# Layer norm on token rows, with the inverse deviation of two norms as a power on GpSimd

## What is computed

```python
def _layernorm(x, axis=-1, eps=1e-05):
    m = jnp.mean(x, axis=axis, keepdims=True)
    v = jnp.var(x, axis=axis, keepdims=True)
    return (x - m) / jnp.sqrt(v + eps)
```

## Time and profile before

| | |
|---|---|
| median of three runs | 309.04 us (308.05 to 309.98) |
| span of the profiled execution | 308.5 us |
| that execution's place among the runs | its span is 0.5 us under their median |
| TensorE busy | 301.2 us, 98%, 3082 matmul records |
| VectorE, ScalarE, GpSimd busy | 188.7, 186.6, 157.2 us |
| chain that ended last | TensorE 91%, VectorE 4%, ScalarE 3% |
| granted TensorE clock, mean | 0.998 |

### The profile page before, as it was taken

How to read it: one execution, slowest core, us unless ns; L and a number is a source line. 1 busy time by engine, 2 the same in 40 slices (tenths; PEclk the granted TensorE clock), 3 DMA queues, 4 the chain that set the end, 5 groups by cost and what they waited for, 6 DMA issues and landing times.

```text
span 308.5 us, 7389 instructions
## 1 busy us (share of the span) xinstructions
PE 301.2 (98%) x3082; PEld 278.5 (90%) x3082; DVE 188.7 (61%) x367; ACT 186.6 (60%) x326; POOL 157.2 (51%) x144
## 2 busy tenths in 40 slices
PE   8999999999999999999999999999999999999895
PEld 7877789999998999989999999999999999987673
DVE  2685255656546778467828775664738496746862
ACT  4486337765536793357698566757567464568651
POOL 6042425863525131747868495867685886100332
PEclk9999999999999999999999999999999999999999
DMA  7969353454302331669584838384757643000002
GB/s 257 405 156 232 70 130 125 138 182 147 115 19 87 119 104 42 212 193 279 188 249 137 263 117 290 107 281 149 272 170 216 212 165 88 21 2 3 0 0 83
DMA packets 32432, 46.49 MB, mean 151 GB/s; under 512 B 6965, under 2 KB 18837, under 8 KB 32394
## 3 DMA queue, kind: packets, MB, share of 16 engines
q1 hardware_dynamic: 29994, 42.16, 43.6%
q0 software_dynamic: 960, 2.43, 2.4%
q10 hardware_dynamic: 1440, 1.38, 1.5%
HBM read 38.22 MB, written 5.71 MB: 142 GB/s over the span
## 4 chain that ended last, share of the span: by engine, by line
PE 91%; DVE 4%; ACT 3%; issue 1%; ACTq 0%; POOL 0%; DVEq 0%; POOLq 0%
PE ps L1638 22%; PE ps L1640 22%; PE ps L1639 21%; PE ps L1994 6%; PE ps L1823 3%; PE ps L1789 3%; PE ps L1660 3%; PE ps L1653 2%; PE ps L1774 2%; PE ps L1668 2%; PE ps L1646 1%; PE ps L1904 1%; PE ps L1868 1%; DVE xn_split L1412 1%; ACT w_hi L809 1%
## 5 line engine op out<-in xcount | busy, mean ns | idle before, releaser
L1638 PE MATMUL ps<-c_region,w_hi 128*128 128x224 f32 (+2 forms) x304 | 88.2, 290 | 0.7 <-DVE c_region L1082 0.7
L1640 PE MATMUL ps<-c_region,w_lo 128*128 128x224 f32 (+2 forms) x304 | 85.3, 281 | 0.0
L1639 PE MATMUL ps<-c_region,w_hi 128*128 128x224 f32 (+2 forms) x304 | 85.2, 280 | 0.0
L560 POOL TENSOR_TENSOR w_lo<-w_stage,w_hi 128x512 fp32r<-128x512 f32 x30 | 48.5, 1635 | 31.1 <-ACT w_hi L809 31.0
L1638 PEld LDWEIGHTS ps<-c_region,w_hi 128*128 128x128 f32 x304 | 58.1, 191 | 1.8 <-DVE c_region L1082 1.2
L1639 PEld LDWEIGHTS ps<-c_region,w_hi 128*128 128x128 f32 x304 | 58.1, 191 | 0.3
L1640 PEld LDWEIGHTS ps<-c_region,w_lo 128*128 128x128 f32 x304 | 58.0, 191 | 0.0
L809 ACT ACTIVATE w_hi<-w_stage 128x1024 fp32r<-128x1024 f32 (+1 forms) x42 | 49.7, 1196 | 2.6 <-DVE v_region L1484 2.6
L1082 DVE TENSOR_TENSOR c_region<-s_region,c_region 128x448 fp32r<-128x448 f32 (+1 forms) x44 | 37.3, 848 | 17.5 <-ACT c_region L936 11.6
L567 POOL TENSOR_TENSOR w_lo<-w_stage,w_hi 128x512 fp32r<-128x512 f32 x28 | 37.9, 1384 | 8.3 <-ACT w_hi L809 8.3
L1638 PE MATMUL ps<-xn_split,w_hi 128*128 128x296 f32 x128 | 40.2, 314 | 0.5 <-DVE xn_split L1082 0.4
(11 more groups left out here) (183 smaller groups left out, 573.4 us busy)
## 6 DMA issues: line engine op xcount, KB each, us to landing
w_stage<-in_w_gate SPq DMA_DIRECT2D x17, 512.0 KB, 4.2
w_stage<-in_w_up SPq DMA_DIRECT2D x17, 512.0 KB, 4.5
w_stage<-in_w_down SPq DMA_DIRECT2D x7, 1024.0 KB
expert_rows<-blank_rows SPq DMA_DIRECT2D x4, 448.0 KB, 3.5
v_region<-in_blocks SPq DMA_DIRECT2D x6, 272.0 KB, 4.0
w_stage<-in_w_down SPq DMA_DIRECT2D x3, 512.0 KB
v_region<-expert_rows SPq DMA_DIRECT2D x1, 1344.0 KB, 8.3
expert_out<-v_region ACTq DMA_DIRECT2D x6, 224.0 KB, 4.4
```

The lines of the kernel that those rows point to most:

```text
L560: w = g.tensor_tensor(wl[:, r], ws[:, r], wh[:, r].bitcast(F32), ALU.subtract)
L1638: mm(o, a_h, b_h, start=start, stop=False)
L1639: mm(o, a_h, b_l, start=False, stop=False)
L1640: return mm(o, a_l, b_h, start=False, stop=stop)
```

## The change

The residual is transposed by TensorE to rows of tokens (`turn_in`, three tiles of 128, 128 and 40 tokens per half, six transposes); VectorE takes mean and variance of each tile with `bn_stats` and `bn_aggr` (`sums`), one number per token and partition, and normalises a tile with one `tensor_scalar` (`normal`). TensorE transposes the rows back (`turn_back`), and VectorE copies them from PSUM (`take_back`, `take_halves`, `take_spread`); `high` and `low` read PSUM directly. In layers 0 and 1 ScalarE's `root` stays, on three columns. In layers 2 and 3 GpSimd adds epsilon and raises to the power -0.5 (`inverse_deviation`), and only one load of the sigmoid table is left. The normalised rows of layer 1 are the token rows that are scattered to the experts, so `turn_tokens` and its copies go. Tokens are tiled by halves, six tiles in place of five (TT = 6, TA = 3), with one more pair of scatters and of fetches. Some steps move: `logits(0, ...)` goes behind `gate_up(0, 0)` and `turn_in(1, 1)`, `take_logits` and `rank_experts` for the first half go into unit 0, the low part of the first half of the shared down weight goes to GpSimd, `back_mul(3)` goes ahead of `sums(2, 0)`, and a DMA of the identity is issued between the two late patch loads.

```diff
-TT = NT // P
-TA = NC // P
+TA = -(-NC // P)
+TT = TA * C
...
+                if i == 0:
+                    sp.dma_start(cb[:, 0:CB_TRI], const[:, 0:CB_TRI]).then_inc(s["d_ident"], 16)
...
             for k in range(KD):
                 if k == 1:
+                    pool.wait_ge(s["dn0_hi"], 1)
+                    for o in range(2 * W1, 2 * W1 + W1 // 2, 512):
+                        d = g.tensor_tensor(wl[:, o:o + 512], ws[:, o:o + 512], wh[:, o:o + 512].bitcast(F32), ALU.subtract)
+                    d.then_inc(s["dn0_lo"], 1)
                     pool.wait_ge(s["gate_mul"], 1)
...
+            def inverse_deviation(L, c):
+                n = nth(L, c)
+                r = slice(n * TA, (n + 1) * TA)
+                pool.wait_ge(s["ln_mv"], (n + 1) * TA)
+                g.tensor_scalar(rstd[:, r], pat(mv[:], n * TA * 2 + 1, [2, TA]), EPS, None, ALU.add).then_inc(s["ln_log"], 1)
+                pool.wait_ge(s["ln_log"], n + 1)
+                g.tensor_tensor(rstd[:, r], rstd[:, r], power[:, 0:TA], ALU.pow).then_inc(s["ln_rs"], 1)
+
+            inverse_deviation(2, 0)
+            inverse_deviation(2, 1)
+            inverse_deviation(3, 0)
+            inverse_deviation(3, 1)
             for c in range(C):
                 for m in range(KD):
-                    pool.wait_ge(s["ln_xn"], 8 + 2 * c + m)
+                    pool.wait_ge(s["ln_xn"], 7 + 2 * c + m)
...
                 scale_second(4)
                 back_silu(3)
+                sigmoid_tables()
+                scale_second(5)
                 back_high(2)
-                square(2, 0)
                 back_high(3)
...
-            log_exp_tables()
-            root(2, 0)
-            sigmoid_tables()
             delta(0, 0)
-            square(2, 1)
-            log_exp_tables()
-            root(2, 1)
-            sigmoid_tables()
             delta(0, 1)
             delta(1, 0)
             delta(1, 1)
-            log_exp_tables()
-            square(3, 0)
-            root(3, 0)
             previous(0, 0)
-            square(3, 1)
             previous(0, 1)
-            root(3, 1)
             previous(1, 0)
             previous(1, 1)
             relu_first(0)
-            sigmoid_tables()
...
+            def sums(L, c):
+                for i in range(TA):
+                    n, j = tokens(i), TA * nth(L, c) + i
+                    dve.wait_ge(s["ln_turn"], C * nth(L, c) + i // 2 + 1)
+                    v.bn_stats(bn[0:n, j * 6:(j + 1) * 6], row_bank(L, c, i)[0:n, :]).then_inc(s["ln_bn"], 1)
+                for i in range(TA):
+                    n, j = tokens(i), TA * nth(L, c) + i
+                    dve.wait_ge(s["ln_bn"], j + 1)
+                    v.bn_aggr(mv[0:n, 2 * j:2 * j + 2], bn[0:n, j * 6:(j + 1) * 6]).then_inc(s["ln_mv"], 1)
...
+                dve.wait_ge(s["ln_rs"], nth(L, c) + 1)
+                for i in range(TA):
+                    n, j = tokens(i), TA * nth(L, c) + i
+                    v.tensor_scalar(row_tile(L, c, i), row_bank(L, c, i)[0:n, :], mv[0:n, 2 * j:2 * j + 1],
+                                    rstd[0:n, j:j + 1], ALU.subtract, ALU.mult).then_inc(s["ln_row"], 1)
+
+            def take_back(L, c):
+                dve.wait_ge(s["ln_back"], nth(L, c) + 1)
+                v.tensor_copy(chunk(xnf[:], c, NT), turned_back(L, c)).then_inc(s["ln_xn"], 1)
...
                 if u == 0:
-                    centre(1, 1)
-                    shared_down_low(0, s["dn0_hi"], s["dn0_lo"])
+                    sums(1, 1)
+                    take_logits(1, 0, TA)
+                    rank_experts(0, TA)
+                    shared_low(0)
                 if u == 1:
-                    shared_low(0)
+                    normal(1, 1)
                     rows(1, 0, TA)
-                    normal(1, 1)
                     shared_low(1)
                 if u == 2:
                     low(1, 1)
+                    take_back(1, 1)
...
-            centre(2, 1)
+            sums(2, 1)
             add_state(0, 0, state(0, 0, inject(0, 0)))
             normal(2, 1)
             add_state(0, 1, state(0, 1, inject(0, 1)))
+            take_halves(1)
             scan10 = state(1, 0, inject(1, 0))
-            centre(3, 0)
+            sums(3, 0)
             in11 = inject(1, 1)
             add_state(1, 0, scan10)
             scan11 = state(1, 1, in11)
             v.memset(pat(xnf[:], 0, [T + 1, KD * B]), 0.0)
+            normal(3, 0)
             add_state(1, 1, scan11)
-            normal_spread(0)
-            centre(3, 1)
+            take_spread(0)
+            sums(3, 1)
             mix(0, 1, 0)
             mix(0, 0, 0)
+            normal(3, 1)
             mix(0, 1, 1)
             mix(0, 0, 1)
-            normal_spread(1)
+            take_spread(1)
...
-            logits(0, TA, 3)
             half_ready(0, 0)
             pe.wait_ge(s["ln_lo"], 3)
             gate_up(0, 0)
-            mean(1, 1)
-            turn_tokens(0)
+            turn_in(1, 1)
+            logits(0, TA, 2)
             gate_up(0, 1)
             positions(0, TA, 2)
-            variance(1, 1)
...
                 if u == 2:
+                    turn_back(1, 1)
                     pe.wait_ge(s["dn0_lo"], 1)
-                    pe.wait_ge(s["xt_ok"], 1)
+                    pe.wait_ge(s["rows_set"], 1)
...
                 gate(0, 0, 0)
-                mean(2, 1)
+                turn_in(2, 1)
                 gate(0, 1, 0)
-                variance(2, 1)
                 gate(0, 0, 1)
                 gate(0, 1, 1)
+                turn_back(2, 1)
                 gate(1, 0, 0)
                 gate(1, 1, 0)
                 gate(1, 0, 1)
-                mean(3, 0)
+                turn_in(3, 0)
                 gate(1, 1, 1)
-                variance(3, 0)
-                mean(3, 1)
+                turn_back(3, 0)
+                turn_in(3, 1)
                 keep_clock(8, 1)
-                variance(3, 1)
+                turn_back(3, 1)
```

More of the change, by code:

```diff
@@ L543, in _ @@
             g.memset(zero[:], 0.0).then_inc(s["const_set"], 1)
-            g.memset(ones[:], 1.0 / D).then_inc(s["const_set"], 1)
+            g.memset(mv[:], 1.0).then_inc(s["const_set"], 1)
+            g.memset(power[:], -0.5).then_inc(s["gap_set"], 1)
             g.memset(eps[:], EPS).then_inc(s["const_set"], 1)
@@ L754, in _ @@
             columns_high(1, 1)
-            square(0, 1)
             columns_high(0, 1)
@@ L818, in _ @@
                 piece_high(n, 0)
-            square(1, 0)
             root(1, 0)
@@ L1145, in _ @@
             patch_low(FULL + 1, 1, SPLIT0 + 2)
-            centre(0, 0)
+            dve.wait_ge(s["const_set"], 2)
+            sums(0, 0)
             patch_low(FULL + 2, 1, SPLIT0 + 3)
             patch_low(FULL + 3, 1, SPLIT0 + 4)
+            normal(0, 0)
             columns_low(2, 1, 1)
@@ L1156, in _ @@
             columns_low(1, 0, 1)
-            centre(0, 1)
+            sums(0, 1)
             columns_low(0, 0, 1)
+            normal(0, 1)
             v_evac(0)
-            normal(0, 1)
             v_evac(1)
@@ L1410, in find_slots @@
                     for st in range(ST):
-                        for b, at, c, n0, n1 in SPREAD:
-                            w = v.tensor_scalar(hot(st, c, n0, n1), bank(b, n1 - n0, at),
+                        for c in range(C):
+                            w = v.tensor_scalar(hot(st, c), bank(4 + c, NC),
                                                 rcb[:, RB_SLOT + st:RB_SLOT + st + 1], None, ALU.is_equal)
@@ L1683, in _ @@
             embed(0, 1)
-            pe.wait_ge(s["const_set"], 3)
+            pe.wait_ge(s["d_ident"], 16)
             pe.wait_ge(s["cls_set"], 1)
-            mean(0, 0)
+            turn_in(0, 0)
             embed(1, 1)
@@ L1718, in _ @@
             value_full(0, 0)
-            mean(0, 1)
+            pe.wait_ge(s["bias_ev"], 1)
+            turn_in(0, 1)
             pe.wait_ge(w_lo[2], 1)
@@ L1724, in _ @@
             value(1, 0)
-            variance(0, 1)
             value(1, 1)
-            pe.wait_ge(s["bias_ev"], 1)
+            turn_back(0, 1)
             pe.wait_ge(s["d_const"], 16)
@@ L1832, in _ @@
             output(0, 1, 0, HP // 2)
-            mean(1, 0)
+            turn_in(1, 0)
             output(0, 1, HP // 2, HP)
-            output(1, 1, 0, 1)
-            variance(1, 0)
-            output(1, 1, 1, HP)
+            output(1, 1, 0, 5)
+            turn_back(1, 0)
+            output(1, 1, 5, HP)
             def gate_up(e, u):
@@ L2129, in gathered_expert, with down_and_turn @@
                     down(3).then_inc(s["g_y"], 1)
-                def variance_and_down():
-                    variance(2, 0)
+                def down_and_turn():
                     back_down(2)
+                    turn_back(2, 0)
                 for e in range(1, NX):
@@ L2142, in _ @@
                 back_gate_up(3)
-                mean(2, 0)
+                turn_in(2, 0)
                 back_down(0)
```

(2 more changed lines are left out.)

277 lines of the change are left out of this document (122 added, 155 removed).

## The result

The changed kernel takes 324.73 us (median of four runs, 323.84 to 328.99) against 308.75 us for the kernel before beside it (four runs): ratio 1.0517, 95% interval 1.047 to 1.0564. The profiled execution took 324.14 us, its span is 322.2 us, 13.7 us more than before. The forecast was 315.3 us, 308.0 to 319.5: the direction was right, the forecast loss of 6.3 us less than half of the measured 16.0.

A forecast was written before the change was run, and what follows sets the result against it. TensorE, busy 98% and 91% of the chain, bounds the kernel, except the last 40 us, where the chain leaves for ScalarE and VectorE. 308.5 + 0.6 (experts) + 5.7 (tail) = 314.8, forecast 315.3 us with 0.5 from span to median; range 308.0 to 319.5.

The forecast's parts named there:

- `mixr_mul` behind the last power: Fourth norm, second half: GpSimd's two first-half products, 1.29 us each, come after the last power and hold the first mix.
- a wait at `positions`: Second layer: TensorE arrives at 107.9 and waits 1.2 us for VectorE's run of work ending at 109.0.
- six table loads: ScalarE's loads of 1.28 us each in the tail shrink to one, off the chain; worth less than they look.
- the drain that the Trainium skill counts: ScalarE table switch: the skill counts 2.66 us with a 1.38 us drain; the prediction saw no drain in the rows.
- rival 1: TensorE's clock falls before the projections: 2 us lost, 317.3 us, up to 319; chance 0.18.
- The pair: GpSimd's add and power on three columns in the third and fourth norm: taken as 0.6 us for both.
- The bound above (2.6 us): Upper bound for GpSimd's add and power together: twice the 1.29 us of a strided 296-wide `tensor_scalar`.
- The third norm's first half: Waits of about 0.65 us (tile 5) and 0.6 us (`normal`) use up TensorE's saving: first gate 0.2 us late.
- the copy behind the state: Third norm, second half: `take_halves(1)` behind the state holds the gates; the last add ends 3.2 us later.
- The second layer: Waits at `positions` and for `rows_set` delay the second logits; +0.6 us at the experts for both layers, bounds -2.0 and +2.0.
- the move of the down weight's split to GpSimd: First half of the shared down weight goes from VectorE to GpSimd, busy 51% of the span: costs nothing.
- The late first call: Under rival 4 (chance 0.10): by the skill, `inverse_deviation(2,0)` would come some 5 us late, sum near 320 us.

The follow-up runs named there:

- the mended kernels: tail_mended, and the changed kernel with ScalarE's roots, copy ahead of the state, GpSimd's split moved and zero matmuls in the waits: 322.42 us, ratio 1.035.
- before_no_keep: The kernel before without its eight zero matmuls between mean(3,1) and variance(3,1): ratio 0.999.
- roots_on_scalar: Changed kernel with logarithm and exponential on ScalarE, with table changes, in place of GpSimd's power: 317.93 us, ratio 1.0365.
- 1, 2, 3 and 6: Experiment numbers of no_pair (ratio 1.0332), roots_on_scalar (1.0365), clock_kept (1.0393) and front_only (1.0148).
- clock_kept: Changed kernel with zero matmuls added in TensorE's waits of the tail: 320.14 us, ratio 1.0393.
- mixr_first: Changed kernel with GpSimd's two mixr_mul products for the first half ahead of the last power: 320.44 us, ratio 1.0376.
- no_pair: Changed kernel without GpSimd's add and power of third and fourth norm, inverse root not computed, for timing alone: 317.86 us, ratio 1.0332.
- front_only: First two layers, tokens, merge and spread as in the changed kernel, third and fourth norm as in the kernel before: 313.31 us, ratio 1.0148.
- tail_mended: Changed kernel with mixr_mul ahead of the last power, copy ahead of the state, GpSimd's split moved, zero matmuls in the waits: 325.42 us, ratio 1.0404.

## Why the prediction fell short

The account, from the two profiles and the mended kernels (us, T to `project(0,3)` unless said):

| part | worked out as | us | predicted |
|---|---|---|---|
| up to the second layer's `turn_in` | 105.39 - 105.26 | 0.1 | 0.2 |
| second layer to T | 164.20 - 162.13 | 2.1 | 0.4 |
| orders on VectorE and GpSimd, clock of the gates | 35.48 - 31.45 | 4.0 | } |
| power in place of roots, orders mended | 31.45 - 29.17 | 2.3 | } 5.7 |
| rows and six-tile layout in place of transposed statistics | 29.17 - 25.16 | 4.0 | } |
| clock of the projections | 13.55 - 12.24 | 1.3 | 0 |

The forecast was 9.7 us short of the measured loss. The table has 7.5 of them: 4.6 us from T to `project(0,3)`, 1.3 in the projections and 1.6 ahead of T.

The first two rows are the weak ones. The first mark lies between 103.4 and 105.5 us in the profiles of kernels that do the same on TensorE up to there, so 0.1 is nothing. And the profile of the kernel before was some 1.6 us longer than its median run; since T to `project(0,3)` is 25.16 us in `before_no_keep` too, this surplus lies most likely ahead of T, and the loss there nearer 4 than 2.2 us; this is an estimate, since no second profile of the kernel before shows it. By the same surplus one step of the sum was wrong that has nothing to do with the change: I added 0.5 us to get from the span to the time, and it is 1.9 us (322.2 to 324.14).

**Right.** The direction and its first reason: VectorE's order takes the place of ScalarE's chain. `bn_stats` three in 1.08 us, `sums` 1.3 us against 1.5; `mixr_mul` behind the last power; `normal` and the copy at about their price; a wait at `positions`; six table loads worth nothing (`roots_on_scalar` has all six and is 4.7 us faster). The load is followed by the logarithm at once again (272.07 + 1.28, then 273.36), so the drain that the Trainium skill counts (ScalarE: Activation LUTs, What ACT_TABLE_LOAD costs) does not show here either.

**Failed step: the clock, priced as a rival alone, came together with the forecast.** I wrote that the largest gap near the end was 0.66 us and that no row shows what a broken stretch does, and left it out of the sum (rival 1 gave 2 us, for the projections alone). But my own steps made waits of 0.6 to 2.7 us. The runs: 1.7 us at the gates, 1.3 us at the projections, and 0.9 to 2.4 us behind `positions` (165.1 to 166.6 us from the second layer's `turn_in` to T in the four profiles of 1, 2, 3 and 6, 164.2 without a fall); `clock_kept` gets 3.8 us back. The falls at the gates and behind `positions` were not in the rival at all. A case that follows from the forecast's own waits belongs in its sum.

**The pair was a mis-sized term**: 1.2 to 2.1 us for 0.6. The bound above (2.6 us) held, the choice near the lower end did not: I scaled with the number of elements, but the power of three columns took 0.88 us or more, longer than the 0.69 us of two operands of 296 columns. At `normal(3,1)` more is lost, since `mixr_mul` waits behind it: `mixr_first` gets 1.6 us of the chain back, `roots_on_scalar` and `no_pair` 5 us with the clock.

**The third norm's first half was the second**: +0.2 us predicted for the first gate. It starts 9.5 us after T instead of 7.2: waits of 0.72 us (tile 5) and 1.31 us (`normal` behind the pair) in place of 0.65 and 0.6, and transposes back of 0.9 us where I took 0.55. Of the 2.3 us 0.65 come with the layout alone (the same mark in `front_only`); I had given merge and spread 0.2 us or less. So the second half's `normal` was late by itself, and the copy behind the state, my largest term (3.2 us), held only 0.7 us.

**The second layer**: the wait at `positions` was 2.0 us for 1.2. I costed the move of the down weight's split to GpSimd at nothing because GpSimd is busy half the time; by moving the next split onto VectorE's ranking it cost 1.1 us there, though only 0.3 us at T. And the work that TensorE was spared became waiting for VectorE.

**The late first call and the transposes.** The first power took 1.78 us and the second 0.88 us, and it started 0.08 us behind the end of the add (272.01 + 0.26, then 272.35): 0.9 us more, nothing hidden. The Trainium skill (GPSIMD Engine Reference, 2.1 Instruction dispatch) gives some 6 us to the first call of a freshly loaded routine; no such delay shows here, and whether a routine was freshly loaded at that point is not known. What stands around a wait does not sort the falls. The clock held at the 1.74 us with matmuls on both sides and, in the three kernels with zero matmuls in the waits of the tail, from the first of them to the end of the projections, but five falls stand behind the 2.0 us at `positions`, which has matmuls on both sides too; and of the pairs of waits with only transposes between them (`turn_back(2,1)`, then the gates) some were followed by a fall and those of `no_pair` and `roots_on_scalar`, 1.2 to 1.7 us each, were not. By the Trainium skill (TensorE: Matmul & The Clock Gate, Part 4: PE-mode transpose) a transpose does not count as TensorE being busy; no run changed the transposes alone, so that it matters here is not shown.

**Open.** Why the clock falls behind a given wait in one execution and not in the next; the runs give only how often. No version with rows beats the kernel before: with everything mended the rows cost 4.0 us in the tail, 0.6 of them by the layout. I put the rest down to each half's chain (in, sums, root, normal, back, copy), which is longer than mean, square and variance were; no run takes it apart further.

## What to carry to other kernels

Where the work that fills TensorE's waits runs out, price a change by the latency of the chain through the slower engines, not by the work it saves TensorE, and add what the clock takes behind the waits that the change itself makes. An add and a power of three columns on GpSimd cost 1.2 to 2.1 us here, and what stands behind them in GpSimd's order waits as well; ScalarE's roots with six table loads, on an idle ScalarE, cost less. Before moving work to an engine with idle time, look at what the other engines do at that moment.

## What the hardware showed unexpectedly

- A power of three columns on GpSimd takes 0.88 to 1.16 us, the first one 1.78 us, in all seven kernels that have it.
- `bn_aggr` of three tiles takes 0.29 us together, `bn_stats` of 256 columns 1.08 us for three; a `tensor_scalar` of 256 columns from PSUM with two per-partition operands 0.53 us, three in 1.44 us.
- GpSimd's subtraction of 512 columns held a VectorE operation with two operands in SBUF for 1.1 us.
- A fall to half clock lasted from 3.4 us (gates of the changed kernel) to 10 us (265 to 275 us in `tail_mended`), behind a single wait up to 6.8 us (`positions` in `clock_kept`). The fall of 3.4 us at the gates cost 1.7 us; of those behind `positions` one of 3.4 us cost 0.9 us and the one of 6.8 us 2.4.
- Zero matmuls in TensorE's waits raised the mean clock of the changed kernel from between 0.963 and 0.983 to between 0.995 and 0.999 in four of five runs, and gave 3.8 us back.
